# Latent attention with a key index on one Trainium2 core: queries placed at a pair's first step, row maxima ahead of low parts, a fifth step of eight turned by DMA in the second pass

## The reference, cut to what matters

```python
xn = _layernorm(x)                                     # x: 1 x 1024 x 512
q_lat = rmsnorm(xn @ q_a_w, q_a_norm_w)                # rank 192
q = (q_lat @ q_b_w)                                    # 32 heads x (128 + 64 rope)
ckv = xn @ kv_a_w                                      # latent 64 + rope 64
kv = rmsnorm(kv_lat, kv_a_norm_w) @ kv_b_w             # 32 heads x (128 + 128)
idx_scores = ...                                       # 16 index heads, causal
mask = top_k(idx_scores, 128) & causal                 # one mask for all heads
scores = (q_nope @ k_nope.T + q_pe @ k_pe.T) * 192 ** -0.5
attn = softmax(where(mask, scores, -inf))
out = (attn @ v) @ o_w
return x + out + experts(xn)                           # 2 of 8 low-rank experts
```

## Time and profile before

| | us |
|---|---|
| median of 3 runs | 929.11 (928.5 to 930.42) |
| the profiled execution's own time | 927.43 |
| its span | 925.6 |
| second pass, units 17 to 29, each | 268.15 / 13 = 20.63 |

### The profile page before, as it was taken

How to read it: one execution, slowest core, us unless ns; L and a number is a source line. 1 busy time by engine, 2 the same in 40 slices (tenths; PEclk the granted TensorE clock), 3 DMA queues, 4 the chain that set the end, 5 groups by cost and what they waited for, 6 DMA issues and landing times.

```text
span 925.6 us, 20231 instructions
## 1 busy us (share of the span) xinstructions
PE 808.1 (87%) x7496; PEld 500.8 (54%) x7496; DVE 674.0 (73%) x1557; ACT 601.8 (65%) x1340; POOL 532.0 (57%) x440
## 2 busy tenths in 40 slices
PE   4979989987768898898888898999999988989998
PEld 2435544444435555565555566666666666664443
DVE  5365678799999999999998777777877777760000
ACT  2656789979886788787887666666766666650000
POOL 3184278877874545545554777777877767650000
PEclk9989999989999999999999999999999999999999
DMA  7012211203443444443542678767576776771211
GB/s 246 24 35 80 80 35 47 85 12 100 121 111 92 136 118 115 124 124 106 140 121 58 109 137 138 139 141 141 121 138 125 120 143 139 150 141 28 69 53 38
DMA packets 168787, 96.67 MB, mean 104 GB/s; under 512 B 116721, under 2 KB 142705, under 8 KB 168689
## 3 DMA queue, kind: packets, MB, share of 16 engines
q1 hardware_dynamic: 168688, 95.37, 44.1%
HBM read 36.62 MB, written 6.29 MB: 46 GB/s over the span
## 4 chain that ended last, share of the span: by engine, by line
PE 46%; DVE 25%; issue 12%; POOL 7%; ACT 7%; DMA 2%; SPq 1%; DVEq 0%; POOLq 0%; ACTq 0%
PE psS L701 12%; PE psS L774 9%; DVE arena L1237 6%; DVE arena L1043 5%; PE psT L758 5%; DVE m L1177 5%; ACT arena L805 4%; DVE bias L1184 4%; PE psT L553 3%; PE psT L573 2%; PE psS L530 2%; POOL arena L1351 2%; PE psO L728 2%; PE psS L586 2%; DVE bias L1128 2%
## 5 line engine op out<-in xcount | busy, mean ns | idle before, releaser
L701 PE MATMUL psS<-keyT,arena 128*128 128x512 f16 (+3 forms) x1152 | 231.1, 329 | 33.0 <-issue 17.9
L992 ACT ACTIVATE arena<-arena,small 128x512 f32<-128x512 f32 (+7 forms) x256 | 198.2, 774 | 70.4 <-DVE small L1242 38.2
L805 ACT ACTIVATE arena<-psT 128x512 f16<-128x512 f32 (+4 forms) x360 | 171.8, 505 | 97.1 <-PE psT L622 43.8
L1043 DVE SCALAR_TENSOR_TENSOR arena<-psT,arena 128x512 f16<-128x512 f32 (+3 forms) x278 | 146.7, 547 | 97.4 <-ACT arena L805 96.6
L1237 DVE CUSTOM_DVE_ANT_0 arena<-psS,bias 128x512 f32<-128x512 f32 (+7 forms) x256 | 191.5, 748 | 1.0 <-PE psS L701 0.6
L701 PEld LDWEIGHTS psS<-keyT,arena 128*128 128x128 f16 x1152 | 91.5, 98 | 89.7 <-issue 23.2
L758 PE MATMUL psT<-ident,arena 128*128 128x128 f32 x736 | 115.6, 278 | 26.8 <-DVE arena L1043 23.9
L586 PE MATMUL psS<-ikT,big 128*128 128x512 f16 (+3 forms) x528 | 104.4, 343 | 22.9 <-DVE bias L1128 19.4
L758 PEld LDWEIGHTS psT<-ident,arena 128*128 128x128 f32 x736 | 84.4, 141 | 60.1 <-ACT arena L992 32.8
L1417 POOL TENSOR_TENSOR bias<-arena,bias 128x768 f32<-128x768 f32 (+2 forms) x48 | 91.4, 1919 | 32.9 <-ACT arena L871 21.7
L1184 DVE MATCH_REPLACE8 bias<-m,bias 128x768 f32<-128x768 f32 (+4 forms) x112 | 89.9, 809 | 0.0
(11 more groups left out here) (164 smaller groups left out, 1382.4 us busy)
## 6 DMA issues: line engine op xcount, KB each, us to landing
arena<-arena SPq DMA_DIRECT2D x192, 128.0 KB, 2.4
arena<-in_wiq SPq DMA_DIRECT2D x32, 256.0 KB, 2.7
arena<-in_ow SPq DMA_DIRECT2D x16, 512.0 KB, 3.5
arena<-in_qbT SPq DMA_DIRECT2D x16, 256.0 KB, 2.5
wvo_parts<-arena SPq DMA_DIRECT2D x16, 256.0 KB, 2.0
arena<-in_qpe SPq DMA_DIRECT2D x16, 128.0 KB, 2.9
arena<-in_x SPq DMA_DIRECT2D x8, 256.0 KB, 3.0
out<-arena SPq DMA_DIRECT2D x8, 256.0 KB, 2.0
```

The lines of the kernel that those rows point to most:

```text
L701: last = mm(bank[:, k:k + w], Q[:, u % 2, h, a, q:q + P], keyT[:, b, h, k:k + w], start=(a, b) == (0, 0), stop=(a, b) == (1, 0))
L805: return nc.scalar.activation(dst, src, ACT.Copy, scale=scale)
L992: nc.scalar.activation(pr[:, g % 4, 0:kw], pr[:, g % 4, 0:kw], ACT.Exp, bias=shift[:, g % 4:g % 4 + 1], scale=-1.0, accum_out=rsum[:, unit ...
L1043: return v.scalar_tensor_tensor(out=dst, in0=src, scalar=scale, in1=hi, op0=ALU.mult, op1=ALU.subtract)
```

## The change

Everything lies in the two passes' loops, and with one exception only in the second.
- `TURNED` for the second pass goes from (1, 3, 5, 7) to (1, 2, 3, 5, 7): tile 4 of head 0 is turned by DMA too. Its column's row sum gets `PR_S` (`scaled[:, 1, 1:2]`, and `eps_ok` counts one more).
- SP calls both `place`s of a unit at s = 0, ahead of `turn`, not at s = 1 and s = 2 behind it. In the first pass there are no turns and nothing else stands between, so the order of SP's DMAs is the old one there.
- POOL does `rope_low` at s = 0 ahead of `rows_lo_`, not behind it.
- DVE, in the second pass, does `row_max(g + 3)` ahead of the low parts of step g (the new `next_max`).

```diff
-TURNED = ((), (1, 3, 5, 7))
+TURNED = ((), (1, 2, 3, 5, 7))
...
             for g in range(STEPS):
                 u, s = divmod(g, 8)
+                if s == 0 and 2 <= u + 1 < NU:
+                    place(u + 1, latent, qa_lo, q_lat, 1)
+                    place(u + 1, turned, q_rot, q_tur, 0)
                 if turns(g):
                     turn(g)
-                if s == 1 and 2 <= u + 1 < NU:
-                    place(u + 1, latent, qa_lo, q_lat, 1)
-                if s == 2 and 2 <= u + 1 < NU:
-                    place(u + 1, turned, q_rot, q_tur, 0)
...
+            def next_max(g):
+                if g == 8 * NP:
+                    for t in GROUPS[2]:
+                        mask(t)
+                    dve.wait_ge(mask_done, 7)
+                if g < STEPS:
+                    row_max(g)
+
             for g in range(AHEAD):
                 row_max(g)
-            dve.wait_ge(eps_ok, 2)
+            dve.wait_ge(eps_ok, 3)
             for g in range(STEPS):
                 u, s = divmod(g, 8)
+                if half_of(g):
+                    next_max(g + AHEAD)
                 for use in uses_of(g):
...
-                if g + AHEAD < STEPS:
-                    if g + AHEAD == 8 * NP:
-                        for t in GROUPS[2]:
-                            mask(t)
-                        dve.wait_ge(mask_done, 7)
-                    row_max(g + AHEAD)
+                if not half_of(g):
+                    next_max(g + AHEAD)
...
             g.memset(scaled[:, 1, 4:8], PR_S).then_inc(eps_ok, 1)
+            g.memset(scaled[:, 1, 1:2], PR_S).then_inc(eps_ok, 1)
...
             for x in range(STEPS):
                 u, s = divmod(x, 8)
+                if s == 0 and 2 <= u + 1 < NU:
+                    rope_low(u + 1)
                 if x + 1 < STEPS and turns(x + 1):
                     rows_lo_(x + 1)
-                if s == 0 and 2 <= u + 1 < NU:
-                    rope_low(u + 1)
```

## The result

| | before | after |
|---|---|---|
| median, us | 929.11 | 923.97 (922.2 to 924.94) |
| profiled execution's span, us | 925.6 | 920.4 |
| second pass, units 17 to 29, each, us | 20.63 | 266.06 / 13 = 20.47 |

The account below looks back on a forecast made before the run. TensorE was taken to set the second pass's pace, afterwards a loop of 18.9 us per unit. Savings of 22.5 (units 17 to 29), 2.3, 2.7 and 1.3 made 28.8: 898.6, as a median 900 us; range 887 to 912.

Parts of the forecast that it names:

- issue: TensorE's wait at a unit's first scores, attributed to late placing of queries; 1.17 us per unit, forecast to go to zero.
- waits for maxima: TensorE's waits for row maxima at s = 3 and s = 7 of the scores; 1.0 us per unit, forecast to go.
- floor of TensorE: Second-pass unit time TensorE alone would need after the change: 18.47 - 0.54 = 17.93 us.
- E: End of POOL's rows of s = 3 in a second-pass unit, from which the loop's steps are timed in us.
- finds a gap: Case where L1255, DVE's reciprocal multiplication, does not wait for POOL: unit 18.6 us, total 896; inside the forecast's 0.50.
- A loop that is longer than either: Second-pass chain from E through DVE maxima, exponential, rope_hi and rope_low back to the rows: 18.9 us per unit.
- Maxima first: DVE's row_max ahead of low parts: saves 1.0 us per unit; low parts wait up to 1.21, covered by two steps.
- POOL alone: Second-pass unit time if POOL set the pace: 17.8 us of work and gaps plus 0.8 swap wait, 18.6.
- POOL loses more: Rival: swap wait keeps its 1.42 and some exponential waits stay; 19.8 us per unit, 913 total; chance 0.20.
- TensorE stays the bound: Rival: the swap lands in time and L1255 finds a gap; unit 17.93 us, total 888; chance 0.14.
- Placing is not the cause: Rival: TensorE still loses 1.17 us per unit at the first scores; unit 19.1, total 905; chance 0.08.
- Slower: Rival: POOL's waits stay at 5.25 us per unit with 2.12 work added; unit 22.75, total 953; chance 0.05.

Follow-up runs that it names:

- e14: Changed kernel; second pass: ACT's exponential of s = 1 and rope_hi ahead of the output's high part at s = 7, query's low part first at s = 5: 909.1 us.
- e16: Changed kernel with reciprocals multiplied one column at a time, swap at s = 2 ahead of the turn, rope_hi ahead of the exponential of s = 1: 884.0 us.
- e1: Changed kernel without the fifth turn and with low parts ahead of maxima again, so the kernel before with placing first alone: 910.8 us.
- e5: Changed kernel with the second pass's reciprocals multiplied one column at a time (128x1), and one such column in the first pass: 902.1 us.

## Why the prediction was wrong

**Right.** The first pass is as before (unit 16 starts at 498.1 and 498.0). The wait called "issue" was the placing: predicted 1.17 per unit, measured 1.1 (20.63 to 19.54). The waits for maxima were predicted at 1.0 and were 0.73 to have. POOL's work was predicted at 17.50 per unit and is 17.46. The floor of TensorE, 17.93, is borne out by units of 18.08. L1255 does wait for POOL in the second pass, from E + 2.4 to E + 4.1, and that is worth 14 us in units 17 to 29. The case that the sum set beside it, 896 if it "finds a gap", was too fast: with the wait gone it is 902, and would be 908 without the 6 us of the first pass.

**Wrong, the main step.** In "A loop that is longer than either" the exponential of s = 1 starts when its maximum is ready. It can't: ACT is in order, and the exponential of s = 0 and the output's high part stand ahead of it. The former waits behind the last high part of s = 6, whose transposes wait for a PSUM bank; the latter waits for TensorE. The predicted chain lists what stands ahead in DVE's queue, instruction by instruction, and nothing of what stands ahead in ACT's. That gap of 2.0 us, less the 0.5 gained before it, makes the 1.5 us by which 20.4 is longer than 18.9. With ACT's order changed and the query's low part first it shrinks to 0.5 (e14), and the loop is 18.90. That this is the forecast to the hundredth is partly luck: up to the maximum the forecast was 0.5 too long, behind it 0.5 too short.

**Wrong, the step that fed it.** In "Maxima first" the low parts wait up to one maximum, covered by the two steps until their values. The values aren't the only ones who wait. A low part also frees a PSUM bank, of which there are two here, and `wait_freed` is who waits: TensorE stood 14.9 us before L757 and 13.2 before L617 in 13 units. No wait of TensorE for a low part stood in the trace before, and only waits that stood there were counted.

**Mis-sized.** POOL alone was put at 18.6. Without the wait of L1255 it measured 19.1 to 19.4, because its wait for the swap was followed by one for `rope_hi`. Unit 30 was to gain 2.7 and gained 0.1: it has no rotation, but it still runs in the loop. Unit 16 gained 3.5 where 2.3 were forecast. The sum of the stretches is 3.5 + 13 x 0.16 + 0.1, less 0.6 behind unit 31's start, 5.1 of a difference in spans of 5.2.

**The rivals.** "POOL loses more" had the right direction (19.8 per unit, 913), but not the waits: that for the swap fell to 0.9 per unit where 1.42 were to stay, those for exponentials went altogether, and the new one, 1.6, is for `rope_hi`. "TensorE stays the bound" is what e16 reaches, at 884 where 888 was said; 7 us of that come from the first pass (unit 16 starts at 491.0). "Placing is not the cause" fell with e1, and "Slower" with the result. The range was too narrow: no case had a wait in ACT's queue or for a PSUM bank in the loop.

## What to carry to other kernels

When a reordering gives an in-order engine more work, write down the chain from its late end back to itself through **every** queue that it passes, with what stands ahead of each instruction there, whatever that engine's share is; then look at who waits for a buffer that the delayed instruction frees. Before adding load to POOL, look for DVE instructions whose longest duration is several times their median, as in the earlier trace rows: such a line can be cheap only because POOL is idle when it comes, as this one was in the second pass before. And measure the parts alone: here two of three made 29 us, and the third took 24 back until three small waits were gone.

## What the runs showed of the hardware

The exclusion of DVE and POOL depends on the form. A 128x8 tensor_tensor with both inputs in SBUF took 0.17 us beside an idle POOL and up to 1.72 beside a busy one; in the second pass of the changed kernel all 16 that took longer ended about 0.02 us after a tensor_tensor of POOL. A 128x4 float32 tensor_scalar was held as long (1.63 in the median, 0.16 in a gap). A 128x1 one was never held (143 to 156 ns in over 200 executions, most of those of e5 beside a busy POOL), nor was a 128x8 reciprocal (0.19 to 0.20 in the 32 of e16, most of them beside a busy POOL). DVE instructions with one input in PSUM kept their durations: the 128x1024 maximum took 1.21 on average before and 1.22 after, and in the changed kernel all 128x512 products of `unit_out` took 0.69. Two and three columns weren't tried. The Trainium skill's page "SBUF — State Buffer", section "Who interferes with whom", says this of instructions with two SBUF inputs and of tensor_scalar where it can enter a two-port mode. For the first the runs agree. For the second they agree in that the 128x4 form was held; which mode it ran in, or why a single column is exempt, no run here shows.
